# Two value projections into the output products' banks, normalising by column halves, and a new order of a round's steps, in a feed-forward and attention kernel on one Trainium2 core

## The reference

```python
x = x + 0.5 * ffn(layernorm(x))            # stage 0: 2 layers x 8 sequences
x = x + attn(layernorm(x))                 # 16 heads of 16 channels, then @ weight
x = x + 0.5 * ffn(layernorm(x))            # stage 1: the same again

def _layer(x, wqkv, qs, ksc, wo, lg, lb, w1, b1, w2, b2):
    q, k, v = split(shift_token(x) @ wqkv)           # 8 heads of 64
    q, k = rotary_xpos(l2norm(q) * qs, l2norm(k) * ksc)
    x = x + local_attention(q, k, v) @ wo            # each block of 128 tokens sees itself and the one before
    h = layernorm(shift_token(x)) * lg + lb
    a, g = split(h @ w1 + b1)                        # 682 columns each
    return x + (a * gelu(g)) @ w2 + b2
```

## Time and profile before

| | us |
|---|---|
| median of 3 runs | 3990.23 (3989.36 to 3994.13) |
| the profiled execution, its time | 3999.0 |
| its span, first to last instruction | 3997.3 |
| TensorE busy | 3751.3 (94%) |
| VectorE busy | 2573.6 (64%) |
| ScalarE busy | 2228.3 (56%) |
| GpSimd busy | 2184.3 (55%) |

### The profile page before, as it was taken

The page is one execution under the profiler, slowest core; times in us unless marked ns, Lnnn a source line. Parts: engine busy times, 40 slices in busy tenths (PEclk is TensorE's granted clock), DMA queues, the critical chain, the costliest instruction groups (busy, mean ns, idle before and its releaser), DMA issues.

```text
span 3997.3 us, 75744 instructions
## 1 busy us (share of the span) xinstructions
PE 3751.3 (94%) x23552; PEld 3063.5 (77%) x23552; DVE 2573.6 (64%) x7286; ACT 2228.3 (56%) x5232; POOL 2184.3 (55%) x2179
## 2 busy tenths in 40 slices
PE   4999999999999799999999999998999999999997
PEld 3777777777777688888888888876777777777776
DVE  5677667766776465565555555656776677766774
ACT  2655665566656455444444444446656665566554
POOL 3555555555655355555555555655555555555653
PEclk8999999999999899999999999999999999999999
DMA  4000001110100100000000010001010011100110
GB/s 141 16 30 27 18 18 51 49 35 24 33 28 29 46 27 22 1 17 7 12 17 2 17 44 1 17 2 50 25 32 18 18 47 53 35 24 24 35 32 25
DMA packets 119072, 114.75 MB, mean 29 GB/s; under 512 B 13181, under 2 KB 116233, under 8 KB 118793
## 3 DMA queue, kind: packets, MB, share of 16 engines
q1 hardware_dynamic: 118792, 111.44, 8.8%
HBM read 73.69 MB, written 29.36 MB: 26 GB/s over the span
## 4 chain that ended last, share of the span: by engine, by line
PE 80%; DVE 10%; issue 4%; POOL 2%; DMA 1%; ACT 1%; SPq 1%; DVEq 0%; POOLq 0%; ACTq 0%
PE psum L1357 20%; PE psum L1358 18%; PE psum L1359 18%; PE psum L1469 6%; PE psum L1479 5%; PE psum L1499 5%; PE psum L1604 3%; PE psum L1458 2%; DVE nrm L1117 2%; DVE nrm L1115 1%; PE psum L1552 1%; DMA nrm<-xmid 1%; PE psum L1517 1%; PE psum L1437 1%; DVE turned_qk L1025 1%
## 5 line engine op out<-in xcount | busy, mean ns | idle before, releaser
L683 POOL TENSOR_TENSOR ge_lo<-ge,ge_hi 128x512 fp32r<-128x512 f32 x512 | 716.2, 1402 | 550.7 <-PE psum L1359 306.4
L643 POOL TENSOR_SCALAR probs<-probs,rz 128x256 f32<-128x256 f32 (+1 forms) x1024 | 444.6, 454 | 526.9 <-DVE rz L1077 526.9
L883 ACT ACTIVATE ge<-psum 128x512 f32<-128x512 f32 x512 | 306.4, 598 | 631.8 <-PE psum L1604 631.7
L789 ACT ACTIVATE probs<-probs,nb,rq 128x256 f32<-128x256 f32 (+1 forms) x1024 | 575.9, 566 | 40.7 <-DVE nb L1071 40.0
L1249 DVE CAST ge_hi<-ge 128x512 fp32r<-128x512 f32 x512 | 244.7, 479 | 546.6 <-ACT ge L883 546.3
L1063 DVE CUSTOM_DVE_ANT_0 probs<-psum,mask 128x256 f32<-128x256 f32 (+1 forms) x1024 | 339.4, 387 | 288.4 <-PE psum L1469 262.7
L625 POOL TENSOR_TENSOR rinv<-ssq,minus_half 128x16 f32<-128x16 f32 x124 | 365.5, 2947 | 162.7 <-DVE ssq L1040 159.2
L1357 PE MATMUL psum<-wqkv_hi,hT_hi 128*128 128x512 f32 x768 | 335.0, 436 | 53.8 <-DVE turned_sin L1029 52.1
L770 ACT ACTIVATE squares<-psum 128x512 f32<-128x512 f32 x256 | 150.2, 599 | 355.8 <-PE psum L1359 234.5
L653 POOL TENSOR_TENSOR hid_lo<-gate,hid_hi 128x512 fp32r<-128x512 f32 x160 | 207.5, 1297 | 254.2 <-ACT hid_hi L821 254.2
L1358 PE MATMUL psum<-wqkv_hi,hT_lo 128*128 128x512 f32 x768 | 308.6, 402 | 0.0
(11 more groups left out here) (163 smaller groups left out, 10579.1 us busy)
## 6 DMA issues: line engine op xcount, KB each, us to landing
xnext<-stream SPq DMA_DIRECT2D x32, 512.0 KB, 4.6
xmid<-stream SPq DMA_DIRECT2D x32, 512.0 KB, 3.8
stream<-xmid SPq DMA_DIRECT2D x16, 512.0 KB, 2.9
nrm<-xmid SPq DMA_DIRECT2D x32, 224.0 KB
wbuf<-L_ffn_wqkv SPq DMA_DIRECT2D x8, 768.0 KB, 8.2
wbuf<-L_ffn_w SPq DMA_DIRECT2D x8, 682.0 KB, 4.4
x_all<-L_attn_x SPq DMA_DIRECT2D x8, 512.0 KB, 7.7
stream<-x_all SPq DMA_DIRECT2D x8, 512.0 KB, 3.9
```

The source lines that it names most:

```text
L643: last = nc.gpsimd.tensor_scalar(pu, pu, rz[:, h, t:t + 1], 1.0, ALU.mult, ALU.mult)
L683: nc.gpsimd.tensor_tensor(ges[1][:, k % 4, :], ge[:, k % 4, :], f32(ges[0][:, k % 4, :]), ALU.subtract).then_inc(S["g_lo"], 1)
L789: last = nc.scalar.activation(pu, pu, ACT.Exp, bias=nb[:, h, t:t + 1], scale=rq[:, 0, t, h:h + 1], accum_out=zs[:, h, t:t + 1])
L883: nc.scalar.activation(ge[:, k % 4, :], RB[k % 2], ACT.Exp, scale=GSCALE, accum_out=gz[:, h, t:t + 1]).then_inc(S["g_exp"], 1)
```

## The change

It has six parts. (1) v0 goes to AV and v1 to UB instead of the two RB banks; v2 and v3 stay there. (2) `j` is split into `j0` (columns 0 to 127, four instructions) and `j1` (columns 128 to 255), and `n0` and `n1` each wait for their own half. (3) All four tables have a new order. (4) VectorE's table begins with `-y0 c3 Y -y1`, which stood at its end as `y0 +Y +c3 y1`; its loop body now ends behind c2. (5) The first q, k, v and the first g wait for each column half of their input apart, and S0 waits for the first two blocks of q and k alone, S1 for the rest. (6) v0 of a round that loads weights waits for the biases. The number of products, copies and transfers stays.

```diff
-PE_STEPS = ("S0 -g3 -a2 S1 -w0 -a3 S2 -g4 T0 S3 -w1 T1 S4 -a4 -w2 T2 A0 S5 A1 T3 S6 -w3 T4 S7 A2 A3 +z0 +z1 -w4 "
-            "-g5 T5 +q0 +k0 A4 T6 +k1 -w5 +q1 A5 W0 T7 A6 +q2 W1 A7 +Q0 +k2 +K0 W2 W3 B +K1 +k3 +Q1 +q3 +Q2 +v0 "
-            "+v1 +v2 n0 n1 +v3 +Q3 g0 a0 +K2 g1 a1 +K3 g2").split()
-
-
-
-ACT_STEPS = ("-G2 -G3 E0 -u2 E1 i0 E2 i2 H0 -G4 H1 E3 i1 -u3 H2 E4 O0 H3 E5 -u4 E6 H4 O1 +zh0 +zh1 E7 -G5 +sq0 H5 "
-             "-u5 +sk0 H6 +sq1 +sk1 H7 O2 f0 +sq2 O3 f1 +Qc0 +Kc0 +sk2 +sk3 +Qc1 +sq3 +vh0 +vh1 +Qc2 +Kc1 nh0 nh1 "
-             "G0 f2 +vh2 +vh3 +Qc3 +Kc2 u0 G1 +Kc3 u1").split()
-
-
-
-DVE_STEPS = ("X0 -y2 X1 R0 X2 i0 R1 L0 X3 i2 -y3 R2 L1 -y4 X4 i1 R3 L2 X5 R4 L3 X6 X7 P0 R5 L4 P1 R6 +zl0 +zl1 L5 "
-             "-y5 +rq0 R7 +rk0 L6 +ss0 -F -e +rk1 +ss1 +rq1 L7 +c0 P2 f0 P3 f1 +rq2 +c1 +rk2 x +ss2 l +rk3 r +rq3 "
-             "j +ss3 nl0 nl1 B +c2 y0 f2 +Y +c3 y1").split()
-
-
-POOL_STEPS = ("-ul1 N0 -ul2 N1 N2 N3 -ul3 N4 -ul4 N5 N6 -ul5 N7 +d0 +p0 +b0 +p1 +b1 +d1 +b2 +d2 +p2 s +b3 +d3 +p3 "
+PE_STEPS = ("S0 -a2 -g3 S1 -w0 -g4 S2 -a3 -w1 S3 T0 -w2 T1 -a4 S4 T2 A0 S5 A1 A2 S6 T3 -w3 S7 T4 A3 -w4 +z0 +z1 "
+            "-g5 A4 T5 +q0 +k0 A5 T6 -w5 +k1 +q1 T7 W0 +q2 A6 W1 A7 W2 +Q0 W3 B +K0 +k2 +v0 +K1 +Q1 +k3 +q3 +v1 "
+            "+Q2 +v2 +v3 n0 n1 +Q3 g0 a0 g1 +K2 a1 g2 +K3").split()
+
+
+
+ACT_STEPS = ("-G2 -G3 E0 -u2 E1 i0 E2 i2 H0 -G4 -u3 H1 E3 i1 -u4 H2 E4 E5 H3 O0 E6 O1 H4 E7 +zh0 +zh1 -G5 H5 +sq0 "
+             "-u5 +sk0 +sk1 H6 +sq1 O2 f0 H7 +sq2 O3 f1 +Kc0 +Qc0 +sk2 +sk3 +vh0 +sq3 +Qc1 +Qc2 +vh1 +vh2 +Kc1 nh0 "
+             "nh1 G0 f2 u0 G1 +Qc3 +vh3 +Kc2 +Kc3 u1").split()
+
+
+
+DVE_STEPS = ("-y0 c3 Y -y1 X0 -y2 X1 X2 i0 R0 -y3 R1 R2 L0 X3 i2 L1 -y4 X4 i1 L2 R3 X5 R4 X6 L3 P0 R5 X7 L4 P1 R6 "
+             "+zl0 R7 +zl1 -y5 L5 +rq0 +rk0 +ss0 -F -e L6 +rk1 +ss1 P2 f0 +rq1 L7 +c0 +c1 P3 f1 +rq2 x l B +rk2 "
+             "+ss2 r +rk3 +rq3 j0 j1 nl0 nl1 f2 +ss3 +c2").split()
+
+
+POOL_STEPS = ("-ul1 -ul2 N0 N1 N2 N3 -ul3 N4 -ul4 N5 N6 N7 -ul5 +b0 +d0 +p0 +p1 +d1 +b1 +d2 +b2 s +d3 +b3 +p2 +p3 "
...
+HEAD_DVE = {0: "Y c3"}
...
-            return {"z": RB[i % 2], "q": RB[3 * i % 2], "k": RB[(3 * i + 1) % 2], "v": RB[(3 * i + 2) % 2],
+            return {"z": RB[i % 2], "q": RB[3 * i % 2], "k": RB[(3 * i + 1) % 2], "v": (AV, UB, RB[0], RB[1])[i],
...
                 if kind == "j":
-                    dve.wait_ge(S["pool_rs"], m + 1)
+                    if i == 0:
+                        dve.wait_ge(S["pool_rs"], m + 1)
+                    half = slice(i * P, (i + 1) * P)
                     for t in range(NT):
-                        V.tensor_scalar(nrm[:, t, 0:P], xmid[:, t, 0:P], mv[:, t, 0:1], rs[:, t:t + 1],
-                                        ALU.subtract, ALU.mult)
-                        last = V.tensor_scalar(nrm[:, t, P:D], nrm[:, t, P:D], mv[:, t, 0:1], rs[:, t:t + 1],
+                        last = V.tensor_scalar(nrm[:, t, half], (xmid, nrm)[i][:, t, half], mv[:, t, 0:1], rs[:, t:t + 1],
                                                ALU.subtract, ALU.mult)
...
             def a_round(n, prev=True, nxt=True, load=None, switch=None, final=0, layer=0):
-                some_steps(n, prev, nxt, None, load, switch, final, layer, table=left(DVE_STEPS, BEGUN_DVE, load))
+                some_steps(n, prev, nxt, None, load, switch, final, layer, 
+                           table=left(DVE_STEPS, {**BEGUN_DVE, **HEAD_DVE}, load))
 
             def last(m, final, call=call):
+                some_steps(m + 1, True, False, -1, final=final, layer=1, part=slice(0, 2))
...
+        if kind == "v" and i < 2:
+            return [("AV", "UB")[i]]
...
-                    if i == 0:
-                        pe.wait_ge(S["dve_z"], KD * (m + 1))
+                    if w == 2 and i == 0 and load is not None and not ahead:
+                        pe.wait_ge(S["bias_ok"], load + 1)
                     for kt in range(KD):
+                        if i == 0:
+                            pe.wait_ge(S["dve_z"], KD * m + kt + 1)
...
                     heads, blocks = unit(i)
-                    if i == 0:
-                        pe.wait_ge(S["act_qt"], NT * (m + 1))
-                        pe.wait_ge(S["act_kt"], NT * (m + 1))
+                    if i < 2:
+                        pe.wait_ge(S["act_qt"], NT * m + blocks[1] + 1)
+                        pe.wait_ge(S["act_kt"], NT * m + blocks[1] + 1)
...
-                    pe.wait_ge(S["dve_n"], m + 1)
+                    pe.wait_ge(S["dve_n"], KD * m + i + 1)
...
-                    if i == 0:
-                        pe.wait_ge(S["dve_nlo"], KD * (m + 1))
                     for kt in range(KD):
+                        if i == 0:
+                            pe.wait_ge(S["dve_nlo"], KD * m + kt + 1)
...
```

More of the change, by code:

```diff
@@ L1222, in last @@
                     variance(0, "g_mv", "g_var")
-                some_steps(m + 1, True, False, -1, final=final, layer=1, part=slice(0, 1))
+                some_steps(m + 1, True, False, -1, final=final, layer=1, part=slice(2, 3))
                 if call == 0:
                     normalise(0, gn, gx[0], "g_rs", "g_y")
-                some_steps(m + 1, True, False, -1, final=final, layer=1, part=slice(1, 3))
+                some_steps(m + 1, True, False, -1, final=final, layer=1, part=slice(3, 5))
                 if call == 0:
                     y_lo(0, 0)
-                some_steps(m + 1, True, False, -1, final=final, layer=1, part=slice(3, 4))
+                some_steps(m + 1, True, False, -1, final=final, layer=1, part=slice(5, 6))
                 if call == 0:
@@ L1232, in last @@
                     pack(0, 0, 0)
-                some_steps(m + 1, True, False, -1, final=final, layer=1, part=slice(4, None))
+                some_steps(m + 1, True, False, -1, final=final, layer=1, part=slice(6, None))
                 stage_end(dve, 1 + call)
```

## The result

| | us |
|---|---|
| before, median of 5 runs beside it | 3990.27 (3989.36 to 3994.13) |
| after, median of 5 runs | 4009.25 (4005.34 to 4016.68) |
| ratio | 1.0048, 95% interval 1.0037 to 1.0059 |
| profiled execution after, its time and its span | 4006.2, 4004.4 |

The change made the kernel 19 us slower, where 60 us of gain were forecast.

A forecast was written before the change was run, and what follows sets the result against it. TensorE, busy 94% of the span, was taken to bound the kernel. Gains of 30 us in layer 0, 24 in layer 1 and 6 in rounds with weights made 60, from the median 3990.2 to 3930; range 3898 to 3985.

The forecast's parts named there:

- The banks: TensorE's projections: v0 and v1 in AV and UB no longer wait, removing some 2.5 us a round with Q2's wait.
- the end of the stretch: TensorE from W3 to g0 in the new order: g0 as if it began 15.6 us behind W3's start.
- The first rival: GpSimd's power beside j1 holds j0 and j1, every one of 30 rounds loses 2.9 us: about 4015, chance 0.06.
- the rival in which the gain does not come: rk2 or ss2 slip ahead of r on VectorE, n0 waits as before, 0 to 10 us remain; chance 0.07.
- 3.0 us saved in the stretch: W3 to g0, each round: a new loss of 1.1 us against the old one of 4.0 to 4.2.
- I take 0.4 off for those that fail: Rest of the round: 0.4 us deducted for covers of 0.1 to 0.3 us, worked out from one round's rows.
- 2.5: Gain in us of each of 12 loop-like layer-0 rounds (3.0 - 0.5), together 30; each layer-1 round gains 2.0, together 24.
- the three places: Rest of the round, cover lost: exponentials and E7 before zh (0.3 left); L6 before T7 (waits 1.0 in layer 1); A2 behind A1.
- Rounds with weights: I take 1.0 each for six of them: First round, last of layer 0 and first of layer 1, in each call: 1.0 us gained each, together 6.
- I expect the slow end in that loop again ... and put it at nothing either way: VectorE's branch in the second call's layer-1 loop: 5.4 us idle, a1 waits about 2, against 1.7 before.
- the rival in which it stands everywhere: All four loops show the 5.4 us in front of y0, 17 other ends cost 2 each: 3965, chance 0.12.
- The slower rival, E7 ahead of zh: ScalarE's chain reaches zh1 late and q0 pays in all 30 rounds; at 3 us late about 4010, chance 0.11.

The follow-up runs named there:

- the two kernels on the banks: Kernel before with the banks alone changed, 1.0070; changed kernel with f0, f2 late and last loop 12 instructions later, v0 and v1 back in RB, 1.0202.

## Why the prediction was wrong

**The banks, and the end of the stretch: right.** The stretch was forecast at 15.6 us and took 15.76. j1 and nl were waited for 0.9 together where 1.1 was put. The first rival is out by the trace: the power (L626) lay beside j1, whose four instructions took 1.10 us, and what held one of j0's to 1.3 us was GpSimd's sum:

```profile
468.24 2.11 DVE L1118 TENSOR_SCALAR nrm<-xmid,mv,rs 128x128 f32<-128x128 f32 x4
470.27 1.10 DVE L1118 TENSOR_SCALAR nrm<-nrm,mv,rs 128x128 f32<-128x128 f32 x4
...
468.46 1.30 POOL L617 TENSOR_TENSOR turned_qk<-turned_qk,turned_sin 128x512 f32<-128x512 f32 x1
469.71 2.91 POOL L626 TENSOR_TENSOR rinv<-ssq,minus_half 128x16 f32<-128x16 f32 x1
```

n0 does not wait in steady rounds, so the rival in which the gain does not come is out too. That v0 and v1 stop waiting is shown by the two kernels on the banks.

**"3.0 us saved in the stretch": 2.7.** The loss of 4.0 to 4.2 us before holds. The idle times shown in it add up to 3.15 (v1 1.46, n0 1.04, Q2 0.37, v0 0.28), but a wait costs more from start to start than the idle time beside it. In the changed kernel n1 starts 1.03 us behind n0, with 0.37 of idle time; in the kernel before the two have no wait between them and take 0.82 together, so n0 alone takes about 0.41 and the wait costs 0.6. The step prices hold too: W3 to n0 was forecast at 13.0 and took 13.14 without a wait. The slip is in what remains. "Without waits it would be at 14.5" does not follow from these prices (13.0 + 0.8 + 0.36 = 14.2), so the new loss was 1.4 and not 1.1 by the forecast's own numbers, and 15.76 - 14.2 = 1.6 as measured.

**"I take 0.4 off for those that fail", "2.5", "2.0 each": 1.5 and 1.0.** This is the step that failed in the steady rounds. The rest of a layer-0 round (all but W3 to g0, K0 and k2) was to lose 0.5 us and lost 1.1: T4 waits 0.49 for what looks like L3, S6 0.16 and W3 0.14; 0.3 us are not taken apart. T4's wait was not among the three places gone through. In layer 1 T7's wait of 1.0 was forecast and came (1.07); the rest of the round was to lose 1.0 and lost 1.6.

**"Rounds with weights: I take 1.0 each for six of them": the wrong sign.** This is the largest miss, 37 us by the profiled executions. I wrote "same waits, more work on VectorE", and did not go through the order of `f0` and `f2`, which the difference of the tables shows, with their length (2.8 and 1.8 us) and their own wait for ScalarE. The rounds 0, 8, 16 and 24 have both waits, 3.1 for L7 and 3.4 for c2, and in five of these eight the clock fell. Moving f0 and f2 back gave 30 us.

**"I expect the slow end in that loop again ... and put it at nothing either way": half right.** The slow end did stay in that loop alone, so the rival in which it stands everywhere is out. But it cost 22 us after and 8 before, and not the same. The wait came to 1.5 to 2.9 us, near the 2 that I had worked out, and the three of 2.7 us and more lowered TensorE's clock for 3 to 4 us, which I had no term for. That "the same branch elsewhere hides in the wait for S0" was wrong: with y0 behind the branch VectorE is idle 0.7 us in the other loops, where no code is fetched.

**The slower rival, E7 ahead of zh: out.** q0 does not wait in steady rounds (three waits for hT in the whole span, 3.4 us); the slowdown came from a mechanism that I had not named.

The sum with what was measured: 17.6 + 1.1 + 2.9 + 2.6 gained and 31.2 lost give 7 us slower for the profiled pair, which is what their spans show. Against the forecast of 60 us gained that is 67 us short: 37 in the rounds with weights, 23 in layer 1 (17 of them in the call with the slow loop), 12 in layer 0, less 5.5 gained elsewhere. The 12 us between that and the medians are the positions of the two profiled executions in their own scatter.

Open: how much of the 31.2 us belongs to the change in an average execution, since the part of the clock differs from one to the next. Rounds 7 and 23 stay longer than before in every kernel with the new order, by 0.5 us and mostly by 1 to 3; no run here takes that apart.

## What to carry to other kernels

In a table of steps, read the rows that are empty in the common round first: a split of 3 us that few rounds have can stand ahead of the one copy that TensorE waits for, and it costs more there than the common round gains. Count what there is to win between the starts of steps, with prices read where nothing waits: a wait costs TensorE more than the idle time shown beside it. Then go through every step that lost its cover, T as well as the projections, since each small wait counts in all rounds. After any edit of a looped body look at the first instruction behind each branch, and take waits that merge into one of 3 us as dearer than the same time in waits of 1.5.
